# Selective scan of a state-space layer: two of every eight products with C move from VectorE to GpSimd

## The reference, cut to what matters

```python
dt = softplus(dbc[..., :1] * dt_w + dt_b)
Bp, Cp = dbc[..., 1:1 + D_STATE], dbc[..., 1 + D_STATE:]

def step(h, inp):
    x_t, dt_t, B_t, C_t = inp
    A_bar = jnp.exp(dt_t[..., None] * A)
    h = A_bar * h + dt_t[..., None] * B_t[:, None, :] * x_t[..., None]
    y_t = jnp.einsum('bdn,bn->bd', h, C_t)
    return (h, y_t)
...
y = jnp.moveaxis(ys, 0, 1) + xc * D
y = y * silu(z)
return y @ W_out + residual
```

## Time and profile before

| | us |
|---|---|
| median of 3 runs | 2512.63 (2509.29 to 2513.92) |
| the profiled execution | 2509.35, span 2507.6 |
| VectorE busy | 1682.1 (67%) |
| TensorE busy | 1985.6 (79%) |
| GpSimd busy | 826.8 (33%) |
| ScalarE busy | 989.2 (39%) |
| from the first load of B to the last product with the gate | 151.15 to 569.54 |

### The profile page before, as it was taken

How to read it: one execution, slowest core, us unless ns; L and a number is a source line. 1 busy time by engine, 2 the same in 40 slices (tenths; PEclk the granted TensorE clock), 3 DMA queues, 4 the chain that set the end, 5 groups by cost and what they waited for, 6 DMA issues and landing times. The chain is left out here.

```text
span 2507.6 us, 37343 instructions
## 1 busy us (share of the span) xinstructions
PE 1985.6 (79%) x10490; PEld 1106.8 (44%) x10490; DVE 1682.1 (67%) x3093; ACT 989.2 (39%) x2104; POOL 826.8 (33%) x603
## 2 busy tenths in 40 slices
PE   5945555557799898776999999978887799974777
PEld 2412222223466666333333333355444455542777
DVE  5769999993777777485555555556432466667994
ACT  2654333330577776225565555511211111111321
POOL 1036666560422220001666666610000022211342
PEclk8979999998899999897999999989989799986888
DMA  1024444441766663200455545353011421126220
GB/s 62 1 91 146 146 133 150 143 133 48 147 135 138 140 140 90 94 30 18 145 164 174 170 142 165 91 184 96 0 32 27 128 93 59 68 90 220 86 81 30
DMA packets 137566, 264.96 MB, mean 106 GB/s; under 512 B 34630, under 2 KB 89831, under 8 KB 134936
## 3 DMA queue, kind: packets, MB, share of 16 engines
q1 hardware_dynamic: 119864, 220.96, 30.0%
q0 software_dynamic: 13824, 37.77, 4.8%
q10 hardware_dynamic: 3808, 5.38, 0.8%
HBM read 214.61 MB, written 49.44 MB: 105 GB/s over the span
## 5 line engine op out<-in xcount | busy, mean ns | idle before, releaser
L552 PE MATMUL mamba_y<-mamba_read,ident 128*128 128x448 f32 x512 | 228.8, 571 | 162.6 <-DVE mamba_read L524 162.6
L500 POOL TENSOR_TENSOR xn<-mamba_u,mamba_b_all 128x896 f32<-128x896 f32 x128 | 263.3, 2078 | 259.7 <-DMA mamba_b_all<-mamba_b 259.7
L517 DVE TENSOR_TENSOR_SCAN mamba_state<-mamba_state,xn 128x896 f32<-128x896 f32 x128 | 258.9, 2023 | 6.5 <-POOL xn L500 6.0
L2378 ACT ACTIVATE moe_w_tile<-moe_w 128x1216 f32 x144 | 175.1, 1217 | 146.1 <-PE moe_y_ps L2330 131.8
L552 PEld LDWEIGHTS mamba_y<-mamba_read,ident 128*128 128x128 f32 x512 | 87.8, 191 | 303.2 <-DVE mamba_read L524 254.2
L2315 PE MATMUL moe_up_ps<-moe_w_tile,moe_xT 128*64 128x352 f32 x1152 | 204.3, 476 | 1.3 <-issue 1.3
L2277 POOL DMA_INDIRECT moe_y<-moe_y_sb,moe_index x144 | 158.0, 1097 | 108.5 <-DVE moe_y_sb L2351 75.6
L963 DVE CUSTOM_DVE_ANT_0 xattn_sm<-xattn_s_ps,xattn_mask 112x375 f32<-112x375 f32 x256 | 138.7, 545 | 80.9 <-PE xattn_s_ps L856 71.3
L1054 ACT ACTIVATE xattn_prob<-xattn_sm,xattn_least 112x375 f32<-112x375 f32 x256 | 154.4, 604 | 74.7 <-DVE xattn_least L963 70.8
L2330 PE MATMUL moe_y_ps<-moe_w_tile,moe_hT 128*64 128x256 f32 (+1 forms) x1152 | 177.3, 403 | 0.0
L2271 POOL DMA_INDIRECT moe_xg<-moe_tok,moe_index x144 | 152.8, 1061 | 53.6 <-issue 37.5
(11 more groups left out here) (310 smaller groups left out, 3931.4 us busy)
## 6 DMA issues: line engine op xcount, KB each, us to landing
moe_w<-moe_w SPq DMA_DIRECT2D x64, 480.0 KB
mamba_b_all<-mamba_b SPq DMA_DIRECT2D x64, 448.0 KB, 3.5
mamba_c_all<-mamba_c SPq DMA_DIRECT2D x64, 448.0 KB, 4.7
soft_w<-soft_w SPq DMA_DIRECT2D x16, 1024.0 KB, 8.4
moe_f_part<-moe_y SPq DMA_DIRECT2D x14, 1024.0 KB, 5.7
soft_logits<-soft_logit SPq DMA_DIRECT2D x28, 512.0 KB, 2.6
soft_logit<-soft_logits SPq DMA_DIRECT2D x14, 1024.0 KB, 5.2
xattn_ks<-xattn_k_parts SPq DMA_DIRECT2D x32, 375.0 KB, 6.5
```

What stands on the lines that cost most here:

```text
L500: pool.tensor_tensor(fed[:, PAIR * s + c], u[:, c0 + c, tok], b_all[:, s], ALU.mult).then_inc(input_ready, 1)
L517: dve.tensor_tensor_scan(state[:, q % 2, 0:HW], state[:, q % 2, 0:HW], fed[:, q % RING], 0.0, ALU.mult, ALU.add).then_inc(state_ready, 1)
L552: mm = pe.matmul(y[:, q % PAIR, w, 0:CW], g.ident[:], read[:, q % 2, w * CW:(w + 1) * CW], start=False, stop=False, skip_group_check=True)
L2378: pipelined(act, SLOT_TILES, RING, [weight_placer(act, 0, lambda to, src: act.activation(to, src, ACT.Copy)), silu, copy_hidden])
```

## The change

- A loop body now holds four rows, eight units (numbered q = 0 to 7), and runs four times per pass. `b_all` and `c_all` are rings of four rows.
- For q = 1 and q = 5 (`BY_POOL`) VectorE's scan writes the state to a new SBUF tile, `kept`, instead of back to PSUM, and GpSimd makes the product with C from it into a new tile, `pool_read`. The other six products of a body stay on VectorE and keep their ring of two, `read`, counted by `out_ready` and `summed`. `pool_out_ready` and `pool_summed` count GpSimd's.
- GpSimd's order in a body: inputs 0 to 4, product 1, inputs 5 to 7, product 5. TensorE adds in the order 0, 2, 1, 3, 4, 6, 5, 7.
- ScalarE, before it refills a slot, waits for the scan alone where GpSimd makes the product, else for VectorE's product.
- SyncE issues the reload of a row of B when GpSimd has made both inputs from it, and the reload of the row of C when both products with it are there, in the order B, C, B, C.

```diff
--- before.py
+++ after.py
@@ -433,71 +433,112 @@
-b_loaded, c_loaded = k.sems("mamba_b_loaded", 2), k.sems("mamba_c_loaded", 2)
+ROWS, PAIR, RING = 4, 2, 4
+UNITS = ROWS * PAIR
+BODIES = NST // ROWS
+passes = [(c0, hh) for c0 in range(0, DIC, PAIR) for hh in range(2)]
+BY_POOL = (1, 5)
+BY_DVE = tuple(q for q in range(UNITS) if q not in BY_POOL)
+PER_POOL, PER_DVE = len(BY_POOL), len(BY_DVE)
+def dve_reads(q):
+    return sum(1 for r in BY_DVE if r <= q)
+def pool_reads(q):
+    return sum(1 for r in BY_POOL if r <= q)
+b_loaded, c_loaded = k.sems("mamba_b_loaded", ROWS), k.sems("mamba_c_loaded", ROWS)
 skip_ready = k.sem("mamba_skip_ready")
 decay_ready, input_ready = k.sem("mamba_decay_ready"), k.sem("mamba_input_ready")
 state_ready, out_ready, summed = k.sem("mamba_state_ready"), k.sem("mamba_out_ready"), k.sem("mamba_summed")
+pool_out_ready, pool_summed = k.sem("mamba_pool_out_ready"), k.sem("mamba_pool_summed")
 y_ready, y_done = k.sem("mamba_y_ready"), k.sem("mamba_y_done")
-PAIR, RING = 2, 4
-UNITS = NST * PAIR
-passes = [(c0, hh) for c0 in range(0, DIC, PAIR) for hh in range(2)]
 with ExitStack() as c2:
-    b_all = k.sb(c2, "mamba_b_all", [P, 2, HW])
-    c_all = k.sb(c2, "mamba_c_all", [P, 2, HW])
+    b_all = k.sb(c2, "mamba_b_all", [P, ROWS, HW])
+    c_all = k.sb(c2, "mamba_c_all", [P, ROWS, HW])
     fed = g.xn[:].rearrange("p h (s t) -> p (h s) t", t=HW)
     never = k.sb(c2, "mamba_never", [P, BPH, 1])
+    kept = k.sb(c2, "mamba_kept", [P, PER_POOL, HW])
     read = k.sb(c2, "mamba_read", [P, 2, HW])
+    pool_read = k.sb(c2, "mamba_pool_read", [P, PER_POOL, HW])
     skip_diag = k.sb(c2, "mamba_skip_diag", [P, DIC, P])
-    def load(sp, row, s):
-        sp.dma_start(b_all[:, s], b_dram[ds(row, 1), :].partition_broadcast(P)).then_inc(b_loaded[s], 16)
-        sp.dma_start(c_all[:, s], c_dram[ds(row, 1), :].partition_broadcast(P)).then_inc(c_loaded[s], 16)
     @block.sync
     def _(sp):
-        for s in range(2):
-            load(sp, s, s)
+        def load_b(row, s):
+            sp.dma_start(b_all[:, s], b_dram[ds(row, 1), :].partition_broadcast(P)).then_inc(b_loaded[s], 16)
+        def load_c(row, s):
+            sp.dma_start(c_all[:, s], c_dram[ds(row, 1), :].partition_broadcast(P)).then_inc(c_loaded[s], 16)
+        for s in range(ROWS):
+            load_b(s, s)
+            load_c(s, s)
+        ROUNDS = 2 * BODIES
         for again in range(2):
-            before = 2 * NST * again
-            with loop(sp, 2 * NST - 2, 2) as n:
-                for s in range(2):
-                    sp.wait_ge(out_ready, 2 + PAIR * (before + n + s + 1))
+            first = 1 if again == 0 else 0
+            with sp.Fori(first, ROUNDS) as r:
+                body = r + (ROUNDS * again - 1)
+                for s in range(ROWS):
+                    sp.wait_ge(input_ready, body * UNITS + PAIR * (s + 1))
                     after_wait(sp, g)
-                    load(sp, n + s + 2, s)
-            if again == 0:
-                for s in range(2):
-                    sp.wait_ge(out_ready, 2 + PAIR * (2 * NST - 2 + s + 1))
-                    load(sp, s, s)
+                    load_b(r * ROWS + s, s)
+                    sp.wait_ge(out_ready, body * PER_DVE + (2 + dve_reads(PAIR * s + 1)))
+                    after_wait(sp, g)
+                    sp.wait_ge(pool_out_ready, body * PER_POOL + (PER_POOL + pool_reads(PAIR * s + 1)))
+                    after_wait(sp, g)
+                    load_c(r * ROWS + s, s)
     @block.scalar
     def _(act):
+        def each(p, c0, tok, r):
+            body = r + p * BODIES
+            for q in range(UNITS):
+                c = q % PAIR
+                if q - 2 in BY_POOL:
+                    act.wait_ge(state_ready, body * UNITS + (RING + q - 1))
+                else:
+                    act.wait_ge(out_ready, body * PER_DVE + (2 + dve_reads(q - 2) if q >= 2 else 2 + dve_reads(UNITS + q - 2) - PER_DVE))
+                act.activation(by_batch[c][:, :, 0:1], never[:], ACT.Exp)
+                src = dt[:, c0 + c, tok].rearrange("p (b l) -> p b l", l=L)
+                act.activation(by_batch[c][:, :, 1:], src[:, :, 1:], ACT.Exp, scale=a_neg[:, c0 + c, ds(r * ROWS + q // PAIR, 1)]).then_inc(decay_ready, 1)
         act.wait_ge(state_ready, RING)
         for p, (c0, hh) in enumerate(passes):
-            tok = slice(hh * HW, (hh + 1) * HW)
-            with loop(act, NST, 2) as n:
-                for s in range(2):
-                    for c in range(PAIR):
-                        act.wait_ge(out_ready, p * UNITS + PAIR * (n + s) + c + 1)
-                        act.activation(by_batch[c][:, :, 0:1], never[:], ACT.Exp)
-                        src = dt[:, c0 + c, tok].rearrange("p (b l) -> p b l", l=L)
-                        act.activation(by_batch[c][:, :, 1:], src[:, :, 1:], ACT.Exp, scale=a_neg[:, c0 + c, ds(n + s, 1)]).then_inc(decay_ready, 1)
+            with act.Fori(0, BODIES) as r:
+                each(p, c0, slice(hh * HW, (hh + 1) * HW), r)
     @block.gpsimd
     def _(pool):
+        def feed(p, c0, tok, r, q):
+            s = q // PAIR
+            if q % PAIR == 0:
+                pool.wait_ge(b_loaded[s], (r + p * BODIES) * 16 + 16)
+            pool.wait_ge(state_ready, (r + p * BODIES) * UNITS + (q + 1))
+            pool.tensor_tensor(fed[:, q % RING], u[:, c0 + q % PAIR, tok], b_all[:, s], ALU.mult).then_inc(input_ready, 1)
+        def read_out(p, r, q):
+            i = BY_POOL.index(q)
+            pool.wait_ge(c_loaded[q // PAIR], (r + p * BODIES) * 16 + 16)
+            pool.wait_ge(state_ready, (r + p * BODIES) * UNITS + (RING + q + 1))
+            pool.wait_ge(pool_summed, (r + p * BODIES) * PER_POOL + (i + 1))
+            pool.tensor_tensor(pool_read[:, i], kept[:, i], c_all[:, q // PAIR], ALU.mult).then_inc(pool_out_ready, 1)
         for p, (c0, hh) in enumerate(passes):
             tok = slice(hh * HW, (hh + 1) * HW)
-            with loop(pool, NST, 2) as n:
-                for s in range(2):
-                    pool.wait_ge(b_loaded[s], 8 * NST * p + 8 * n + 16)
-                    for c in range(PAIR):
-                        pool.wait_ge(state_ready, p * UNITS + PAIR * (n + s) + c + 1)
-                        pool.tensor_tensor(fed[:, PAIR * s + c], u[:, c0 + c, tok], b_all[:, s], ALU.mult).then_inc(input_ready, 1)
+            with pool.Fori(0, BODIES) as r:
+                for q in range(5):
+                    feed(p, c0, tok, r, q)
+                read_out(p, r, 1)
+                for q in range(5, UNITS):
+                    feed(p, c0, tok, r, q)
+                read_out(p, r, 5)
     @block.vector
     def _(dve):
@@ -507,25 +548,25 @@
         dve.memset(never[:], -BIG).then_inc(state_ready, RING)
         dve.memset(read[:, :, 0:1], 0.0).then_inc(out_ready, 2)
+        dve.memset(pool_read[:, :, 0:1], 0.0).then_inc(pool_out_ready, PER_POOL)
+        dve.memset(kept[:, :, 0:1], 0.0).then_inc(pool_summed, PER_POOL)
         for p, (c0, hh) in enumerate(passes):
-            with loop(dve, NST, 2) as n:
-                q0 = p * UNITS + PAIR * n
-                def scan(q):
-                    dve.wait_ge(decay_ready, q0 + q + 1)
-                    dve.wait_ge(input_ready, q0 + q + 1)
+            with dve.Fori(0, BODIES) as r:
+                body = r + p * BODIES
+                for q in range(UNITS):
+                    dve.wait_ge(decay_ready, body * UNITS + (q + 1))
+                    dve.wait_ge(input_ready, body * UNITS + (q + 1))
+                    if q in BY_POOL:
+                        i = BY_POOL.index(q)
+                        dve.wait_ge(pool_out_ready, body * PER_POOL + (i + 1))
+                        dve.tensor_tensor_scan(kept[:, i], state[:, q % 2, 0:HW], fed[:, q % RING], 0.0, ALU.mult, ALU.add).then_inc(state_ready, 1)
+                        continue
                     dve.tensor_tensor_scan(state[:, q % 2, 0:HW], state[:, q % 2, 0:HW], fed[:, q % RING], 0.0, ALU.mult, ALU.add).then_inc(state_ready, 1)
-                def read_out(q):
-                    if q % PAIR == 0:
-                        dve.wait_ge(c_loaded[q // PAIR], 8 * NST * p + 8 * n + 16)
-                    dve.wait_ge(state_ready, q0 + q + RING + 1)
-                    dve.wait_ge(summed, q0 + q + 1)
-                    dve.tensor_tensor(read[:, q % 2], state[:, q % 2, 0:HW], c_all[:, q // PAIR], ALU.mult).then_inc(out_ready, 1)
-                for q in range(2 * PAIR):
-                    scan(q)
-                    read_out(q)
+                    j = BY_DVE.index(q)
+                    dve.wait_ge(c_loaded[q // PAIR], body * 16 + 16)
+                    dve.wait_ge(state_ready, body * UNITS + (RING + q + 1))
+                    dve.wait_ge(summed, body * PER_DVE + (j + 1))
+                    dve.tensor_tensor(read[:, j % 2], state[:, q % 2, 0:HW], c_all[:, q // PAIR], ALU.mult).then_inc(out_ready, 1)
             dve.wait_ge(y_ready, p + 1)
```

(21 more changed lines are left out.)

## The result

| | before | after |
|---|---|---|
| median us | 2513.28 (4 runs, 2509.29 to 2516.82) | 2488.19 (4 runs, 2485.74 to 2494.06) |
| profiled execution, span | 2509.35, 2507.6 | 2486.40, 2484.3 |
| first load of B to the end of the last product with the gate | 418.4 | 395.3 |
| VectorE busy, whole span | 1682.1 | 1643.7 |
| TensorE busy, whole span | 1985.6 | 2017.3 |

The ratio is 0.9909, 95% interval 0.989 to 0.9928: faster by 0.9%. The forecast said 2485 (2476 to 2498). The profiled execution fell by 22.95 us, to 2486.40, where the sum said 27.7 and 2481.7. The scan's stretch (151.5 to 546.8 us) fell by 23.1, so the whole difference lies there.

What follows compares the result with a forecast made beforehand. VectorE was taken to bound the scan. The terms -35.8 + 8.2 - 2.9 + 2.8 = -27.7 us turn the profiled 2509.35 into 2481.7, or 2485 for the median, range 2476 to 2498.

Steps and rivals of the forecast that it cites:

- VectorE bounds the scan: In the scan VectorE is the bound, busy 99.76 of 102 us in pass 3; GpSimd's idle time costs nothing by itself.
- Products taken: Scan: 32 products leave VectorE, the next scan starts 1.94 us later where a unit took 3.065; gain 35.8 us.
- The moved wait: VectorE's other 96 products: wait for the scan moves to a sequencer instruction, 0.085 us each, cost 8.2 us.
- Late inputs: Scans that started late because GpSimd's input waited for a load of B: they go, gain 2.9 us.
- the moved wait costs nothing: Rival for VectorE's 96 products: the 8.2 us fall out of the sum, giving 2476.8 us; chance 0.12.
- What was costed at nothing: Terms put at 0: ScalarE (cover 0.7 us), eight queued loads at the start, C's row 0 reloaded in time.
- GpSimd: Ten GpSimd instructions a body, 2.03 us apart, take 20.4 of 22.8 us; cover 2.1 us at the tightest place, cost 0.
- GpSimd as the bound: Rival: from 2.45 us an instruction the gain is gone; at 2.7 the kernel takes 2535 us; chance 0.05.
- TensorE's clock at the end of a pass: Longer TensorE idle stretches (3.3 us) can lower its clock, so the last add of a pass comes late; cost 2.8 us.
- four ends, one in three hit, and half of it made up: How the pass-end cost was sized: 4.2 us at a hit end, giving 2.8 us; ends of the range 0 and 17.
- the clock falls in most bodies: Rival: TensorE's clock is low at every pass end, 17 us instead of 2.8, total 2499; 0.16 including other small VectorE losses.
- the signs that were named for "wrong": Scan: idle before scans by GpSimd or ScalarE, before products by TensorE, over 2.5 us before the gate, clock far below 0.98.

Runs made afterwards that it cites:

- the last kernel: Changed kernel with a masked weight wait in the routed experts, plus ten small matmuls a body without the start flag: 2533.91 us beside 2555.01, ratio 0.9914.
- the control: Changed kernel with one more register instruction per tile in the routed experts (masked expert number before a wait): 2486.01 us, ratio 0.9879.
- the two mends: On the control, the scan's wait put back on the product and add 5 before add 6: 2515.56 us beside 2554.65, ratio 0.9847.

## Why the prediction was right, and where a term was off

**VectorE bounds the scan: right.** The whole gain is VectorE's, and the forecast of 2485 stands 3 us from 2488. Against the profiled executions, on which the sum was made, it is 4.7 us off (2481.7 and 2486.40), which is nearly all the term of TensorE's clock below; the medians are kinder by chance.

**Products taken: right.** -36.3 against -35.8; the distance after such a scan is 1.930 where 1.94 was worked out from the gate's products. The scan into SBUF takes 2012 ns, not more than into PSUM (2016), so the upper end from the GRU's scan was not needed.

**The moved wait: right, and shown.** 8.0 against 8.2 in the trace, and the kernel that puts the wait back on the product wins 8.7 us. The rival "the moved wait costs nothing" (0.12) is out: with the wait on the instruction the distance is 2.054 for a scan of 2.02, with the wait on the sequencer ahead of it 2.143. The pair in the soft experts had told this. The sentence of the Trainium skill ("VectorE: DVE Perf Modes", "The DRAIN you can't avoid") that the semaphore costs nothing extra does not hold for a wait on the sequencer. Whether it holds for one on the instruction no run here shows, since none has a dependent pair without a wait; independent instructions follow a scan after 1.93.

**Late inputs: right.** -2.8 against -2.9, and the rings alone give 3.5 of stretch. What was costed at nothing (ScalarE, the start, the loads of C) shows no wait.

**GpSimd: right.** 20.3 of 22.8 us, 2.08 a piece. The rival on the slower side, GpSimd as the bound (0.05), needed 2.45 us an instruction; a body of that length was made with two spare products (24.4), and there 6.7 of the 23.1 us were left, where the prediction had nothing left from 24.5 on.

**TensorE's clock at the end of a pass: the mechanism was right, the size was not.** The step that failed is "four ends, one in three hit, and half of it made up", 2.8 us. It measured 8.2: all four ends were hit, at 1.5, 2.6, 1.5 and 2.6 us each. The idle stretch of 3.3 us was in the text (the trace has 3.29 or 3.30 in 21 places of the scan), but one in three was taken from the change of pass, with 2.31 idle, and did not carry over. "Half of it made up" was about right: 4.2 was worked out for an end with all adds at the lower level, and 2.05 is the mean. The rival "the clock falls in most bodies" (0.16 with its neighbours) had the frequency right, a granted clock of 0.81 instead of 0.98, and the price wrong: it took 4.2 for each end, since it let adds 6, 5 and 7 all run at the lower level, where the clock in fact rose during add 5. Half of the four ends' 17 us came true, and the time lies between both cases. Two of the signs that were named for "wrong" did appear, 4.60 us without work before the gate and a clock far below 0.98; the total stayed in its range because this term is small beside the first.

That the clock and not the order or the queue alone makes the ends late is shown by the ends at 3.07 in the same order (the third of the kernel with the wait on the product, two of the last kernel), and by four at 3.07 with small matmuls in between. What decides in a given body whether the clock falls stays open: the ends that came right differ from run to run. The length of the idle stretch just before does not tell it alone: in the kernel with the wait on the product it was 1.82 us at the end that was on time and 3.13 to 3.21 at the three others, but in the last kernel it was 2.24 at all four, two of them on time.

## What to carry to other kernels

Look at which instruction a wait ends up on, not only at how many waits there are: put last the one that comes last, so that the instruction that uses the value holds it (8.7 us for two lines exchanged; with one end of a pass on time as well, 2476 instead of 2486 us). Taking work off an engine that bounds a loop also thins the work of the ones behind it, so TensorE's clock can fall; that costs nothing inside a pass, where it has room, but at each point where someone waits for the last of its matmuls it must be priced at the lower level, and the first work in the queue there should be what is ready first. If a bound engine is relieved by another, count the other's instructions per turn: here one more cost 2.3 us and two cost 17.1 of the 23.1 that the change gives.

## What the runs showed of the hardware that was not expected

- The same two waits in the other order, with the same instructions, change the distance from a scan of 2.02 us to the product from 2.143 to 2.054 us.
- TensorE's granted clock fell from 0.98 to 0.81 in the scan although it had the same matmuls to do in less time, when idle stretches of 1.29 us became stretches of 3.3 us with longer work between. Ten 62-column matmuls a body, each 0.12 us apart, raised it from 0.80 to 0.90 in the control, and from 0.87 to 0.95 (1.00 around an end of a pass) with the two mends.
- A matmul with the start flag in unread columns spoiled the output (relative error 0.37); without the flag the sum is whole.
